# Transposes of probabilities joined in pairs in TensorE's order

## The reference, cut to what matters

```
def _tc_rmsnorm(x, t, gw, gb, bw, bb):
    g = (t @ gw.T + gb)[:, None, :]
    b = (t @ bw.T + bb)[:, None, :]
    inv_rms = jax.lax.rsqrt(jnp.mean(x * x, axis=-1, keepdims=True) + EPS)
    return g * x * inv_rms + b
...
    attn = jnp.einsum('blhd,bmhd->bhlm', q, k) / scale      # 16 heads of 16 channels
    p = jax.nn.softmax(attn, axis=-1)
    o = jnp.einsum('bhlm,bmhd->blhd', p, v).reshape(B, L, D)
    return o @ Wo.T
...
    return jax.nn.silu(x @ gate_w.T) * (x @ hid_w.T) @ out_w.T      # 1024 hidden channels
...
x = x + _attention(_tc_rmsnorm(x, t, g1w, g1b, b1w, b1b), Wq, Wk, Wv, Wo)
return x + _swiglu(_tc_rmsnorm(x, t, g2w, g2b, b2w, b2b), gate_w, hid_w, out_w)
```

## Time and profile before

| What | Value |
|---|---|
| runs | 991.04, 990.25, 996.09 us; median 991.04 |
| profiled execution | span 991.4 us; no other time of it is recorded |
| TensorE busy | 954.4 us (96%), weight loads beside it 817.3 (82%) |
| VectorE busy | 661.2 us (67%) |
| ScalarE busy | 561.7 us (57%) |
| GpSimd busy | 447.6 us (45%) |
| mean granted clock of TensorE | 0.983 |
| transposes of probabilities | L1151, 512 of them, median 272 ns each |
| copies of them on ScalarE | L472, 128, mean 589 ns |
| sums of a pair on VectorE | L771, 128, mean 673 ns |

### The profile page before, as it was taken

One profiled execution on the slowest core, in us unless ns is written; L12 is line 12 of the kernel. 1 busy time (PEld: TensorE's weight loads), 2 busy tenths in 40 slices (PEclk: granted clock), 3 DMA queues, 4 the chain that ended last, 5 costly groups with the idle time before them and its releaser, 6 DMA issues.

```text
span 991.4 us, 24429 instructions
## 1 busy us (share of the span) xinstructions
PE 954.4 (96%) x9112; PEld 817.3 (82%) x9112; DVE 661.2 (67%) x1178; ACT 561.7 (57%) x1271; POOL 447.6 (45%) x393
## 2 busy tenths in 40 slices
PE   6679999999999999999999999999999999999788
PEld 5568888889888898888889888888978888897767
DVE  3856777676777757676675767667576776757552
ACT  6645556565655655565465566646556565655342
POOL 4355345254534535454453545435354552535242
PEclk9688999999999999999999999999999999999999
DMA  5100010000100000010000101000010100000000
GB/s 183 45 1 22 2 38 8 22 21 0 42 0 22 20 21 21 0 42 0 21 21 5 37 0 42 0 21 21 0 42 0 42 0 21 21 0 22 2 22 22
DMA packets 18971, 21.71 MB, mean 22 GB/s; under 512 B 640, under 2 KB 18240, under 8 KB 18816
## 3 DMA queue, kind: packets, MB, share of 16 engines
q1 hardware_dynamic: 18720, 21.24, 6.4%
q10 hardware_dynamic: 224, 0.10, 0.1%
HBM read 12.95 MB, written 8.39 MB: 22 GB/s over the span
## 4 chain that ended last, share of the span: by engine, by line
PE 90%; DVE 3%; ACT 2%; POOL 2%; issue 2%; DMA 1%; DVEq 0%; POOLq 0%; ACTq 0%
PE ps L1051 10%; PE ps L1053 9%; PE ps L1052 9%; PE ps L1143 7%; PE ps L1200 6%; PE ps L1184 6%; PE ps L1151 6%; PE ps L1203 5%; PE ps L1201 5%; PE ps L1192 5%; PE ps L1185 5%; PE ps L1173 3%; PE ps L1077 3%; PE ps L1080 3%; PE ps L1078 3%; PE ps L1069 2%
## 5 line engine op out<-in xcount | busy, mean ns | idle before, releaser
L264 POOL TENSOR_TENSOR h_lo<-h,h_hi 128x512 fp32r<-128x512 f32 x128 | 165.3, 1291 | 251.8 <-ACT h_hi L462 251.8
L270 POOL TENSOR_TENSOR probs<-probs,recip 128x512 f32<-128x512 f32 x128 | 132.8, 1047 | 48.0 <-DVE recip L776 47.8
L1051 PE MATMUL ps<-out_w_hi,h_hi 128*128 128x256 f32 x512 | 150.1, 293 | 0.9
L1053 PE MATMUL ps<-out_w_hi,h_lo 128*128 128x256 f32 x512 | 144.6, 282 | 0.0
L1052 PE MATMUL ps<-out_w_lo,h_hi 128*128 128x256 f32 x512 | 144.2, 282 | 0.0
L799 DVE SCALAR_TENSOR_TENSOR shared<-shared,ps 128x512 f32<-128x512 f32 x128 | 87.4, 683 | 74.9 <-ACT shared L457 74.3
L457 ACT ACTIVATE shared<-ps 128x512 f32<-128x512 f32 x128 | 76.8, 600 | 100.0 <-PE ps L1192 96.4
L1184 PE MATMUL ps<-xn_hi,gate_w_hi 128*128 128x512 f32 x256 | 108.9, 425 | 1.2 <-ACT xn_hi L431 0.8
L1200 PE MATMUL ps<-xn_hi,hid_w_hi 128*128 128x512 f32 x256 | 106.1, 414 | 0.1
L1051 PEld LDWEIGHTS ps<-out_w_hi,h_hi 128*128 128x128 f32 x512 | 96.6, 189 | 11.7 <-POOL h_lo L264 7.3
L472 ACT COPY probsT<-ps 128x512 f32<-128x512 f32 x128 | 73.7, 589 | 56.1 <-PE ps L1151 55.5
(11 more groups left out here) (92 smaller groups left out, 2152.6 us busy)
## 6 DMA issues: line engine op xcount, KB each, us to landing
x_in<-in_x SPq DMA_DIRECT2D x16, 512.0 KB, 3.4
out<-result SPq DMA_DIRECT2D x15, 512.0 KB, 3.0
shared<-in_attT SPq DMA_DIRECT2D x1, 1024.0 KB, 6.8
shared<-in_gateT SPq DMA_DIRECT2D x1, 1024.0 KB, 8.7
shared<-in_hidT SPq DMA_DIRECT2D x1, 1024.0 KB, 4.8
shared<-in_outT SPq DMA_DIRECT2D x1, 1024.0 KB, 6.8
out<-result SPq DMA_DIRECT2D x2, 256.0 KB, 2.2
result<-in_modT SPq DMA_DIRECT2D x1, 256.0 KB, 4.8
```

The source lines that it names most:

```text
L264: nc.gpsimd.tensor_tensor(h_lo[:, j % KEPT, :], h[:, j % 2, :], h_hi[:, j % KEPT, :].bitcast(F32), ALU.subtract).then_inc(h_lo_done, 1)
L270: nc.gpsimd.tensor_tensor(own, own, recip[:, p % TOGETHER, :].unsqueeze(2).to_broadcast([P, SEQS, L]), ALU.mult).then_inc(divided, 1)
L1051: nc.tensor.matmul(dst, a_hi, b_hi, start=first, stop=False, skip_group_check=skip)
L1053: return nc.tensor.matmul(dst, a_lo, b_hi, start=False, stop=last, skip_group_check=skip)
```

## The change

Only TensorE's list in `iteration` changes, at three places. T0 moves from ahead of the gate product of chunk 3 to behind the hidden product of chunk 3, directly ahead of T1. T2 moves from between the gate and the hidden product of chunk 4 to behind them, directly ahead of T3. T4 moves behind the first q product of the next tile, and T5 from behind the first k product to ahead of it, so that T4 and T5 stand together between the two. T6 and T7 stood together already. No instruction is added or removed, and no wait is changed in its count.

```
@@ -1357,20 +1357,17 @@
                     down(u, 0)
                     gate(u, 2)
                     hid(u, 2)
-                if attend:
-                    transpose_probs(t, 0)
                 if mlp:
                     gate(u, 3)
                     hid(u, 3)
                 if attend:
+                    transpose_probs(t, 0)
                     transpose_probs(t, 1)
                 if mlp:
                     gate(u, 4)
+                    hid(u, 4)
                 if attend:
                     transpose_probs(t, 2)
-                if mlp:
-                    hid(u, 4)
-                if attend:
                     transpose_probs(t, 3)
                 if mlp:
                     gate(u, 5, probs_of=t if attend else None)
@@ -1397,14 +1394,13 @@
                     hid(u, 6)
                     down(u, 2)
                     down(u, 3)
+                if ahead:
+                    project_q(t + 1, 0)
                 if attend:
                     transpose_probs(t, 4)
-                if ahead:
-                    project_q(t + 1, 0)
+                    transpose_probs(t, 5)
+                if ahead:
                     project_k(t + 1, 0)
-                if attend:
-                    transpose_probs(t, 5)
-                if ahead:
                     project_q(t + 1, 1)
                 if attend:
                     transpose_probs(t, 6)
```

More of the change, by code:

```diff
@@ L1399, in iteration @@
                     down(u, 3)
+                if ahead:
+                    project_q(t + 1, 0)
                 if attend:
                     transpose_probs(t, 4)
[L1402 to L1405, removed]
                     transpose_probs(t, 5)
                 if ahead:
+                    project_k(t + 1, 0)
                     project_q(t + 1, 1)
```

## The result

The changed kernel takes 1042.89 us (median of 4 runs, 1039.28 to 1043.98). Against the kernel before, run beside it, the ratio is 1.050, with a 95% interval of 1.048 to 1.052: 5% slower. The forecast was 1035, between 1018 and 1058.

What follows compares the result with a forecast made beforehand. TensorE, busy 58.18 of 58.25 us a tile, was taken as the bound, so added waits lengthen the tile. 2.67 + 0.48 = 3.15 us a tile, x 14 = 44 us on 991.4, gave 1035 us, between 1018 and 1058.

Steps and rivals of the forecast that it cites:

- Joining saves nothing: At each of three places, two transpose groups joined cost 1.33 us against 1.34 single; the saving was taken as nothing.
- T0 covered the wait for silu 2: Ahead of gate 3: moving T0 away gives back nothing and leaves a TensorE wait of 0.42 us for silu 2.
- The path to gate 4: T0, its copy, h_hi 2, tanh 3, silu 3, gate 4: gate 4 starts at 502.80, TensorE idle some 2.2 us.
- The four steps behind the copy: Copy of T0 to h_hi 2 0.49, to tanh 3 0.52, to silu 3 0.63, to gate 4 0.74 us.
- T2 costs nothing; gate 5 without a wait: T2 behind hidden 4 costed at nothing; gate 5 follows T2 and T3 at 506.48 instead of 503.81, +2.67 us.
- T4, T5 and the k product: Behind the first q product: the k product waits for ScalarE's copy of T4, so T6 starts 0.48 us later.
- T7 covered by 0.3 us: At T6 and T7: pair 7's division ends about 524.05, before T7 wants it at 524.32, so no wait.
- the second term (0.48): The +0.48 us a tile from moving T4 and T5 around the first q and k products.
- The clock rival: In each tile the new wait brings one half-clock stretch, losing at most 1.70 us: 1059 us; chance 0.15.
- One of its signs of being wrong: The forecast is wrong if the granted clock in the steady tiles falls from 1.00.
- Given back: Rival: existing TensorE waits shrink or T0's copy comes sooner, leaving 1.8 us a tile, 1016 us; chance 0.12.
- not slower: Rival: T0's copy holds nothing up, tanh 3 done under hidden 3, 0.45 us a tile, 998 us; chance 0.06.

Runs made afterwards that it cites:

- with the k product moved: Kernel before with only T4 and T5 moved, plus the first k product put behind the second q product: 1003.16 us, ratio 1.010.
- With a wait of 1.54 us: Changed kernel with the copy of T0 on ScalarE one place later, behind h_hi of chunk 2, still ahead of tanh 3: 1031.13 us, ratio 1.038.
- the longest case: Changed kernel with the exponential of pair 2 on ScalarE moved behind the copy of T0, wait 2.57 us: 1053.19 us, ratio 1.060.

## Why the prediction was right

The direction, the cause and the sizes of the parts hold. Point by point:

- **Joining saves nothing.** Confirmed: T2 with T3 alone leaves the tile within 0.03 of 58.25, where the sum had 0.01.
- **T0 covered the wait for silu 2.** Forecast 0.42. Gate 3 starts 1.82 after hidden 2 (522.78 - 520.96), where six passes take 1.39, so 0.43; the bracket shows 0.25 of it, as the modelled end of hidden 2 reaches into the wait.
- **The path to gate 4.** Forecast 3.01 from T0 to gate 4 (499.79 to 502.80); measured 3.09 (525.68 to 528.77). The four steps behind the copy came as in their rows (0.49, 0.52, 0.63, 0.74); the mis-sized one is the first, from T0 to its copy, taken as 0.63 from T4, here 0.71. Why it is longer is open: behind T4 and T5 joined it is 0.63 again (548.35 to 548.98).
- **T2 costs nothing; gate 5 without a wait.** Confirmed. From hidden 2 to gate 5 the tile lost 2.76 us (11.49 against 8.73), forecast 2.67; nearly all of the difference is the late copy.
- **T4, T5 and the k product.** Forecast 0.48, measured 0.58. T5 waits for its division and the copy of T4 decides, as foreseen; the mis-sized term is the signal from the copy to the k product, taken as 0.05 from a silu and a gate product, here 0.15. Why it is longer is open; with the k product moved, the v product goes on 0.06 after the copies end (529.72 + 1.07 to 530.85). That the wait would be put down to ScalarE's copy did not come: the profile puts it down to "issue".
- **T7 covered by 0.3 us.** Confirmed: T6 and T7 go as one group of 0.79.
- **Sum.** Forecast 3.15 a tile, measured 3.31, so 46.3 us instead of 44 over 14 tiles. The prediction's own range of 1019 to 1045 does not quite follow from its terms: half a microsecond a tile is 7 us and the second term (0.48) 6.7, so 1022 below; above it is 1049, or 1045 if only the 0.2 of idle time is doubled.
- **The clock rival** had 0.15 and came in part. Two tiles of fourteen have a half-clock stretch and take 63.13 and 63.16, 3.2 us together. The forecast price, at most 1.70 a tile, holds (1.6), but that the wait lies nearer to the stretch that kept 1.00 was right for twelve tiles only. One of its signs of being wrong, a granted clock under 1.00 in the steady tiles, thus showed in those two (0.97). A fall in every tile came in no run here.
- **Given back, or not slower:** neither came. Of the 2.76 and 0.58 all but 0.03 is in the tile, so nothing behind absorbed the delay.

The predicted 1035 is 8 us under the median. By the trace, 50.2 us were added to the span: 46.3 in the fourteen tiles by the waits, some 3 by the clock in two of them, and 0.8 in the first and last tile of the kernel together. Some 2 us more come from the base: the forecast set the median against the span of 991.4, but what lies around a span is about 2 us (1043.6 against 1041.6).

## What to carry to other kernels

Where each engine works a fixed list, moving a step on one engine moves a wait on another: look up where the step's consumer stands in its own engine's list, and what stands behind it there. A short step between two products may be there to cover the latency of a third engine; ask what it hides before joining it with its like. An order is only good together with the other lists, and moving the copy of T0 by two places on ScalarE took back 30 of the 51 us.

## What the runs showed of the hardware that was not expected

An idle wait that repeats in every tile brings the lower clock in some tiles only. In the changed kernel all steady tiles have the same wait in front of gate 4, and two of fourteen fall to the 1.2 GHz level behind it, each for one stretch. Ahead of the wait TensorE makes the eight transposes of T0 and T1. This is the first such tile, whose gate 4 passes take 0.63 instead of 0.39, and the stretch of the clock with it:

```profile
153.18 1.04 PE L1151 MATMUL ps<-consts_sb,probs 128*128 128x128 f32 x8
156.27 0.79 PE L1184 MATMUL ps<-xn_hi,gate_w_hi 128*128 128x512 f32 x1 [2.05 <-DVE shared L799]
156.86 0.63 PE L1185 MATMUL ps<-xn_hi,gate_w_lo 128*128 128x512 f32 x1
```

```profile
156.20:159.60 3.40, 3.33 (x8) 2.66 (x9) 1.50 (x4) 1.77 (x9) 2.27 (x3) 0.50 0.00 0
```

With a wait of 1.54 us no steady tile fell, with 2.05 two (and four with T0 moved alone), with 2.57 six; each count is of one execution. In the longest case five of the falls stand at regular places, 157.7, 345.5, 533.2, 720.9 and 908.7, every third tile, and one more at 92.9, in the first of the fourteen. With T0 moved alone they stand at 154.8, 339.1, 584.9 and 830.6, three and four tiles apart. The Trainium skill ("TensorE: Matmul & The Clock Gate", "What's actually happening") says that the chip's watch on TensorE's activity runs on its own and does not start with the kernel. That falls come at some tiles only, and in the longest case mostly at even distances, agrees with it; that it is the cause was not tested here.
